# Two steps of a scatter-accumulate tail: rows read back and summed on VectorE instead of added by the DMA

## The reference, cut to what matters

```
x = x + experts4(layernorm(x), token_ids)
h = layernorm(x)
scores = softmax(h @ G)                      # 8 experts
value, indices = top_k(scores, 2)
out = sum over the two chosen e of value_e * (down_e @ (silu(gate_e @ h) * (up_e @ h)) + lora_B_e @ (lora_A_e @ h))
x = x + out
```

## Time and profile before

| what | value |
|---|---|
| median of 3 runs | 305.5 us (303.59 to 309.94) |
| the profiled execution's own time | 307.53 us |
| its span, first to last instruction | 305.8 us |
| TensorE busy in the span | 267.6 us (88%), 1664 matmuls |
| VectorE busy | 227.6 us (74%) |
| ScalarE busy | 156.2 us (51%) |
| GpSimd busy | 157.0 us (51%) |
| DMA traffic | 45.97 MB, mean 150 GB/s |

### The profile page before, as it was taken

One profiled execution on the slowest core, in us unless ns is written; L12 is line 12 of the kernel. 1 busy time (PEld: TensorE's weight loads), 2 busy tenths in 40 slices (PEclk: granted clock), 3 DMA queues, 4 the chain that ended last, 5 costly groups with the idle time before them and its releaser, 6 DMA issues. The chain is left out here.

```text
span 305.8 us, 6176 instructions
## 1 busy us (share of the span) xinstructions
PE 267.6 (88%) x1664; PEld 227.3 (74%) x1664; DVE 227.6 (74%) x699; ACT 156.2 (51%) x383; POOL 157.0 (51%) x157
## 2 busy tenths in 40 slices
PE   0779979999999999999986978999599999999910
PEld 0457768888888888888865866878399999999700
DVE  8888958689898898888978657577569976767500
ACT  4634434445444544445424355444346678888810
POOL 3651525533388548840584635246324447676760
PEclk9999999999999999999999899799879999999975
DMA  6588998111142214410136462787455658999830
GB/s 265 208 286 241 255 384 259 37 36 36 34 146 85 71 34 150 165 34 2 58 147 226 161 211 76 228 268 239 131 164 178 198 140 138 219 216 137 104 49 0
DMA packets 23279, 45.97 MB, mean 150 GB/s; under 512 B 4540, under 2 KB 8636, under 8 KB 22656
## 3 DMA queue, kind: packets, MB, share of 16 engines
q0 software_dynamic: 9488, 21.84, 26.9%
q1 hardware_dynamic: 13760, 23.74, 26.1%
HBM read 24.49 MB, written 25.80 MB: 164 GB/s over the span
## 5 line engine op out<-in xcount | busy, mean ns | idle before, releaser
L446 POOL DMA_INDIRECT out<-pair_out,dest_now x37 | 49.0, 1324 | 35.3 <-DVE pair_out L1024 14.9
L528 ACT ACTIVATE aT_hi<-p_aT 128x512 fp32r<-128x512 f32 x19 | 11.4, 599 | 50.0 <-PE p_aT L1193 44.3
L1287 PE MATMUL p_y<-ctx_hi,aT_hi 128*128 x76 | 32.5, 428 | 1.8 <-DVE rec L826 1.8
L1288 PE MATMUL p_y<-ctx_lo,aT_hi 128*128 x76 | 30.8, 405 | 0.0
L406 POOL TENSOR_TENSOR rstd<-var_eps,neg_half 128x1 f32<-128x1 f32 x19 | 12.7, 666 | 34.1 <-DVE var_eps L795 34.0
L1287 PE MATMUL p_h<-ctx_hi,xT_hi 128*128 x72 | 29.9, 416 | 0.0
L1288 PE MATMUL p_h<-ctx_lo,xT_hi 128*128 x72 | 28.4, 394 | 0.0
L399 POOL DMA_INDIRECT xin<-x,gather_row x19 | 20.5, 1081 | 13.6 <-DVE rec L826 9.2
L423 POOL DMA_INDIRECT rows_a<-rec,dest x19 | 18.9, 997 | 14.6 <-DVE dest L902 5.2
L423 POOL DMA_INDIRECT rows_b<-rec,dest x19 | 18.8, 991 | 5.5 <-issue 5.5
L1394 PE MATMUL p_y<-down_hi,aT_hi 80*128 x44 | 21.3, 485 | 0.0
(11 more groups left out here) (311 smaller groups left out, 783.1 us busy)
## 6 DMA issues: line engine op xcount, KB each, us to landing
whole<-ctx_t SPq DMA_DIRECT2D x4, 1024.0 KB, 5.9
pair_x_late<-rows_b SPq DMA_DIRECT2D x13, 258.0 KB
pair_x_early<-rows_a SPq DMA_DIRECT2D x10, 258.0 KB
whole<-w_up SPq DMA_DIRECT2D x4, 576.0 KB, 7.2
rows_a<-pair_x_early SPq DMA_DIRECT2D x8, 258.0 KB
rows_b<-pair_x_early SPq DMA_DIRECT2D x8, 258.0 KB
pair_x_late<-rows_a SPq DMA_DIRECT2D x8, 258.0 KB
pair_x_early<-rows_b SPq DMA_DIRECT2D x7, 258.0 KB
```

The lines of the kernel that those rows point to most:

```text
L446: nc.gpsimd.indirect_dma_start(out=out, out_offset=bass.IndirectOffsetOnAxis(ap=rows, axis=0), in_=pair_out[:, s % ORING, :], in_offset=No ...
L1287: nc.tensor.matmul(to, hi(i), w_hi(i), start=(i == 0), stop=False)
L1288: nc.tensor.matmul(to, hi(i), w_lo(i), start=False, stop=False)
```

## The change

The last two steps of phase B, s = 42 and 43, no longer add in the DMA. GpSimd reads their rows of the output back into SBUF (read_back, an indirect gather) in its list after store(35) and after store(38), that is three steps apart; VectorE adds the mean to them (add_mean) and later computes p_o * GATE + rows (back_finish), in place of ScalarE's evict; the stores of these two steps are plain. Each of the two steps is a group of its own in GROUPS, so that the list ends [35 to 38], [39, 40, 41], [42], [43] (numbers 11 to 14), and its DEST column is taken at the end of VectorE's iteration i = after + 2, where after is the step in BACK_AFTER: 37 and 40.

```diff
+BACK = 2
+BACK0 = PAIRS - BACK
+BACK_AFTER = {35: 42, 38: 43}
...
-        if s in (EARLY, PHASE) or len(groups[-1]) == 4 or s % ARING in (0, EARLY - XSLOTS, EARLY):
+        if s in (EARLY, PHASE) or s >= BACK0 or len(groups[-1]) == 4 or s % ARING in (0, EARLY - XSLOTS, EARLY):
...
+            def read_back(s):
+                pool.wait_ge(dest_taken, group_of(s) + 1)
+                nc.gpsimd.indirect_dma_start(
+                    out=rows_back[:, s - BACK0, :], out_offset=None, in_=out,
+                    in_offset=bass.IndirectOffsetOnAxis(ap=dest_now[:, s - EARLY:s - EARLY + 1], axis=0),
+                    bounds_check=TOKENS - 1, oob_is_err=False,
+                ).then_inc(back_landed[s - BACK0], 16)
...
             def store(s):
 
                 if s < PHASE:
                     pool.wait_ge(pair_done, s + 1)
+                elif s < BACK0:
+                    pool.wait_ge(evicted, s - PHASE + 1)
                 else:
-                    pool.wait_ge(evicted, s - PHASE + 1)
+                    pool.wait_ge(back_done, s - BACK0 + 1)
...
-                    compute_op=ALU.bypass if s < PHASE else ALU.add,
+                    compute_op=ALU.add if PHASE <= s < BACK0 else ALU.bypass,
...
             for s in range(PAIRS):
                 store(s)
+                if s in BACK_AFTER:
+                    read_back(BACK_AFTER[s])
...
-                if PHASE <= i - 2 < PAIRS:
+                if PHASE <= i - 2 < BACK0:
                     evict(i - 2)
...
+            def add_mean(s):
+                dve.wait_ge(back_landed[s - BACK0], 16)
+                rows = rows_back[:, s - BACK0, :]
+                nc.vector.tensor_scalar(rows, rows, pair_meta(s, MEAN), None, ALU.add).then_inc(back_ready, 1)
+
+            def back_finish(s):
+                dve.wait_ge(stored[s % ORING], 16 * (s // ORING))
+                dve.wait_ge(back_ready, s - BACK0 + 1)
+                dve.wait_ge(o_ready, s + 1)
+                nc.vector.scalar_tensor_tensor(pair_out[:, s % ORING, :], p_o[s % 2][:], pair_meta(s, GATE),
+                                               rows_back[:, s - BACK0, :], ALU.mult, ALU.add).then_inc(back_done, 1)
...
+                if i - 2 >= BACK0:
+                    back_finish(i - 2)
                 if i + 2 < PAIRS:
                     lo2(i + 2)
+                if BACK0 <= i - 1 < PAIRS:
+                    add_mean(i - 1)
                 for group in GROUPS:
-                    if group[-1] == i + 2:
+                    if i == next((after + 2 for after, back in BACK_AFTER.items() if back == group[-1]), group[-1] - 2):
                         take_dest(group)
```

More of the change, by code:

```diff
@@ L62 @@
 TAKEN_OFF = range(2, EARLY)
+BACK = 2
+BACK0 = PAIRS - BACK
+BACK_AFTER = {35: 42, 38: 43}
+assert set(BACK_AFTER.values()) == set(range(BACK0, PAIRS))
 def phase(s):
@@ L83, in group_of @@
     return next(i for i, g in enumerate(GROUPS) if s in g)
-assert (ARING - EARLY) * ROW <= E1 * CTX and ORING * D <= E1 * CTX
+assert (ARING - EARLY) * ROW <= E1 * CTX and (ORING + BACK) * D <= E1 * CTX
 UP_PIECES = 2 * KB
@@ L104, in sem @@
             return stack.enter_context(nc.semaphore(name))
-        with nc.sbuf_tensor("pair_out", [P, ORING, D], F32) as pair_out:
-            pass
+        with nc.sbuf_tensor("results", [P, ORING + BACK, D], F32) as results:
+            pair_out, rows_back = results[:, 0:ORING, :], results[:, ORING:ORING + BACK, :]
         with nc.sbuf_tensor("whole", [P, E1 * CTX + KB * E2 * 2 * UP + E2 * D], F32) as whole:
@@ L270, in build @@
         o_ready, pair_done = sem("o_ready"), sem("pair_done")
+        back_landed = [sem(f"back_landed{i}") for i in range(BACK)]
+        back_ready, back_done = sem("back_ready"), sem("back_done")
         minus_ready, rest_ready, rest_out = sem("minus_ready"), sem("rest_ready"), sem("rest_out")
@@ L1390, in down @@
                     pe.wait_ge(pair_done, s - 1)
+                elif s < BACK0 + 2:
+                    pe.wait_ge(evicted, s - 1 - PHASE)
                 else:
-                    pe.wait_ge(evicted, s - 1 - PHASE)
+                    pe.wait_ge(back_done, s - 1 - BACK0)
                 to = p_o[s % 2][:]
```

## The result

The changed kernel takes 309.37 us (median of 6 runs, 308.51 to 311.95), the kernel before 305.43 beside it (6 runs, 303.59 to 309.94). The ratio is 1.0121, 95% interval 1.0079 to 1.0163, so 2.4 to 5.0 us more, less than 2%. The profiled execution took 309.7, its span is 307.9.

The account below looks back on a forecast made before the run. GpSimd's issue list from step 39 on was taken as the bound; 2.62 us from the held first read-back plus 0.13 after the last issue made 2.75, on a median of 305.5, so 308.25 us, range 304.0 to 311.0.

Parts of the forecast that it names:

- What bounds the kernel: End of the span: GpSimd's issues from step 39 on set the end, at 1.86 to 1.92 us pitch from step 40.
- The wait in front of the first read-back: GpSimd after step 35's store: read-back held until iteration 39's taking, starting at 283.03 not 280.36; list ends 2.62 us later.
- Issue time alone, nothing won or lost: GpSimd's list without the wait: two read-backs at 1.30 us, plain stores 1.15 less, end within 0.1 of before.
- VectorE costs nothing: VectorE's end: two add_mean at 0.61 us and two back_finish fit in idle time or after TensorE's work; cost nothing.
- Landing of the second read-back: Ahead of step 43's store: lands 4.8 us after its start at 289.88, before the 295.8 needed, so no bound.
- the rival: Ahead of back_finish(43): read-back lands later than 5.9 us after issue and sets the end, 310.4 to 311.9; chance 0.10.
- Contention on issue: GpSimd issues beside VectorE's add_mean: nothing added, though the skill page's rule would give up to 1.2 us in all.
- After the last issue: End of GpSimd's queue: a plain store's landing adds between 0 and 0.3 us, taken as 0.13; the 8.22 behind unchanged.
- my rival about it: Final drain: its 7.58 us might depend on adds in flight; if it fell wholly away, 300.7 us; chance 0.04.
- That the change moves no traffic here: Stores of steps 42 and 43: they carry no rows, so the change removes no traffic, only trades issue time and waits.

Follow-up runs that it names:

- Renumbering: Changed kernel with groups numbered in the order of taking, so the first read-back waits only for its own column; 307.38 us beside 306.81 before, ratio 0.9956.
- earlier read-backs: Changed kernel with groups numbered as taken and read-backs after steps 33 and 35 instead of 35 and 38; 295.46 us beside 293.94 before, ratio 1.0055.
- second read-back late: Changed kernel with groups numbered as taken and the second read-back after step 41's store instead of 38's; 308.63 us beside 305.54 before, ratio 1.0126.
- 41 steps: Steps 41 to 43 left out of before and of the changed kernel (groups numbered as taken, change on steps 39 and 40); 289.84 and 289.73 us.
- groups as taken, again: Second measurement of the changed kernel with groups numbered in the order of taking; 306.24 us beside 305.54 before, ratio 1.0028.

## Why the prediction was right

Forecast 308.25, measured 309.37; forecast 2.75 us more, measured 3.12 in the tail, 3.94 between the medians and 2.4 to 5.0 by the ratio. The mechanism is shown; the 0.8 by which the medians differ more than the tail isn't explained by it.

- **What bounds the kernel** (GpSimd's list from step 39 on): shown. Each edit of that list, by itself, moved the end by what it changed in the list: from the last issue's end to the end of the span there are 9.34 to 9.54 us in eleven of the twelve profiles with 44 steps, and 9.90 in the one with eight more gathers, whose drain is 0.53 longer.
- **The wait in front of the first read-back**: the step that decided. Read-back foreseen 4.52 us after step 35's store started, seen at 4.59. Renumbering took it away: 2.74 of the list, where the prediction has 2.66 (2.62 and the 0.04 that issue time alone gives back).
- **Issue time alone, nothing won or lost** (-0.04 in the list): +0.35. A read-back holds the list 1.37 to 1.39, not 1.30; a plain store took 1.03 and 1.01, not 0.98; adding stores after a read-back come 1.86 to 1.90 apart, not 1.85. These make 0.47 of the list's 20.95 against the 20.48 foreseen.
- **VectorE costs nothing**: right. add_mean took 0.51 and 0.59 (0.61 taken). The first began in the idle time foreseen and al2(43) wasn't held by it.
- **Landing of the second read-back**: 4.8 foreseen, 4.0 seen (289.08 to 293.07), so no bound; the rival needed 5.9. Moved by three stores it became the bound.
- **Contention on issue**, priced at nothing: right for the changed kernel, not in general. There the first add_mean began 0.05 before the second read-back, which took 1.07 (the other, beside none, 1.08); the second began 0.72 into the store of step 40, which took 1.57. But in all three places of these kernels where an adding store was issued 0.10 to 0.20 after an add_mean had begun, it took 1.71, 1.80 (both with earlier read-backs) and 1.71 (second read-back late), 0.15 to 0.24 more. The Trainium skill's "SBUF — State Buffer" ("Who interferes with whom") has whichever of the two engines issues first hold the other for its whole instruction, where a tensor_scalar runs in a two-port mode; the adding stores go that way, by less than add_mean's 0.48, and the read-back doesn't.
- **After the last issue**: 0.13 for a plain store's landing. It wasn't there (1.46 us to the drain, 1.53 before). In its place the drain grew by 0.16, because there are two more indirect DMAs. From the last issue's end to the end of the span there are 9.46, 9.43 before: the term came to 0.03 and not 0.13, and that it is no further off is luck, since neither part was foreseen. I had left the drain's 7.6 us as given, and my rival about it asked for the wrong dependence, on the adds in flight.
- **That the change moves no traffic here**: right; both kernels move 45.97 MB. With the empty steps left out, it gains 0.67.

## What to carry to other kernels

A semaphore that several steps of a producer raise in turn counts events, not names: when one of them is moved ahead in time, number the waits by the new order, or the one who wanted it early waits for all that it overtook. Price a wait or an added issue in an in-order queue against the slack that is left until the queue becomes the bound, and spend that slack only once: here the same wait cost 1.3 us alone and 2.7 beside the read-backs. And ask of a step at the end whether it carries data at all before crediting a cheaper transfer.

## What the runs showed of the hardware

- GpSimd's drain at the end of the block is not constant. It took 7.331, 7.494, 7.576, 7.657 and 7.739 us with 3 fewer, 1 fewer, the same, 1 more and 2 more indirect DMAs than before, 0.082 for each, and 0.066 for each of eight gathers issued in the first layer. It was the same to the nanosecond in runs with the same number.
- An indirect DMA of 128 rows holds GpSimd 1.54 to 1.62 when it adds (but for the three told above), 1.00 to 1.04 when it is plain in this place, 1.07 to 1.09 as a bounds-checked gather. It doesn't matter whether a row is in bounds: the two plain stores took 1.04 and 1.01 with rows (41 steps), 1.03 and 1.01 empty.
- An adding store can also hold VectorE. In six places an add_mean began 0.51 to 0.79 after an adding store had: it took 0.50 to 0.78 and ended 1.29 to 1.31 after the store's start each time, as if it could only begin at 0.82 (an estimate: 1.30 less its usual 0.48). Begun 0.32 after one, or 0.84 and more, it took 0.48 or 0.49. This comes from comparing rows and wasn't tried by itself. One of the six, from the kernel "groups as taken, again", timelines of both engines:

```profile
287.43 1.59 POOL L472 DMA_INDIRECT out<-results,dest_now  x1 [0.31 <-issue]
...
287.99 0.75 DVE L1058 TENSOR_SCALAR results<-results,pair_x_early 128x512 f32<-128x512 f32 x1
```

- The chip seems to matter more than all of these edits: before took 305.4 us beside the first result, and 306.8, 305.5 and 293.9 on three chips after it (medians). The changed kernel has the same tail on a slower and on the faster one, 30.41 and 30.47, but its step 35 starts 12.46 earlier on the faster. Of these, 7.2 come between the stores of steps 8 and 13, which start 17.59 apart in the slower profile (211.27 to 228.86) and 10.37 in the faster (205.84 to 216.21). Two stretches of the slower one and one of the faster (columns as in the earlier trace rows):

```profile
215.00:220.00 5.00, 2.73 (x11) 2.16 (x12) 2.75 (x8) 2.42 (x7) 1.55 (x2) 0.76 0.34 109
220.00:225.00 5.00, 5.00 (x23) 4.39 (x22) 3.14 (x10) 1.65 (x5) 1.96 (x2) 0.56 0.62 186
```

```profile
210.00:215.00 5.00, 5.00 (x40) 4.65 (x39) 4.59 (x13) 3.25 (x10) 3.65 (x4) 1.00 0.54 183
```

In the slower one TensorE has gaps first (busy 2.73 of 5 us) and is then granted 0.56 of 2.4 GHz (a mean over time at 2.4 and at 1.2), with 23 matmuls in 5 us; in the faster one it is busy throughout, at 1.00, with 40. Why it has gaps on the one and not on the other wasn't tried.
